# A conditioned transformer block: a second buffer for the turned blocks, the second MLP weight in four transfers, and the turning one step later on VectorE

## What is computed

```python
def rmsnorm(x, w):
    return x * rsqrt(mean(x * x, axis=-1, keepdims=True) + 1e-6) * w

def film(x, cond, w, b):
    scale, shift = split(cond @ w + b, 2, axis=-1)
    return x * (1.0 + scale[:, None, :]) + shift[:, None, :]

h = film(rmsnorm(x, norm1_w), cond, film1_w, film1_b)
Q, K, V = h @ q_w + q_b, h @ k_w + k_b, h @ v_w + v_b
attn = softmax(einsum('bnd,bmd->bnm', Q, K) * D ** -0.5)
x = x + (einsum('bnm,bmd->bnd', attn, V) @ proj_w + proj_b)
h = film(rmsnorm(x, norm2_w), cond, film2_w, film2_b)
out = x + gelu(h @ mlp_w1 + mlp_b1) @ mlp_w2 + mlp_b2      # hidden width 1024
```

## Time and profile before

| | |
|---|---|
| median of 3 runs | 243.05 us (243.01 to 243.99) |
| profiled execution, its own time | 245.84 us |
| its span | 244.1 us |
| PE busy | 222.2 us, 91% of the span |
| DVE busy | 140.1 us, 57% |
| ACT busy | 110.2 us, 45% |
| POOL busy | 70.1 us, 29% |
| granted TensorE clock, mean | 0.991 |
| DMA, over the span | 26.72 MB, 109 GB/s |

### The profile page before, as it was taken

One profiled execution on the slowest core, in us unless ns is written; L12 is line 12 of the kernel. 1 busy time (PEld: TensorE's weight loads), 2 busy tenths in 40 slices (PEclk: granted clock), 3 DMA queues, 4 the chain that ended last, 5 costly groups with the idle time before them and its releaser, 6 DMA issues.

```text
span 244.1 us, 3839 instructions
## 1 busy us (share of the span) xinstructions
PE 222.2 (91%) x1380; PEld 196.9 (81%) x1380; DVE 140.1 (57%) x276; ACT 110.2 (45%) x207; POOL 70.1 (29%) x102
## 2 busy tenths in 40 slices
PE   0987999998899996699999799999999999999994
PEld 0767888967778785699799689999999999999994
DVE  1498766666687863688888865224451454234223
ACT  3157653325433340444336558154746454644440
POOL 1575751004335110445524232510152025200000
PEclk9999999999999999799999999999999999999999
DMA  6993000065554594466466640000200020002002
GB/s 173 353 409 143 3 1 0 32 215 187 172 177 169 173 230 162 157 198 194 142 202 206 218 106 0 3 0 1 86 3 0 0 86 0 0 4 86 0 0 89
DMA packets 15282, 26.72 MB, mean 109 GB/s; under 512 B 1825, under 2 KB 10017, under 8 KB 15009
## 3 DMA queue, kind: packets, MB, share of 16 engines
q1 hardware_dynamic: 15264, 26.50, 33.3%
HBM read 16.00 MB, written 10.49 MB: 109 GB/s over the span
## 4 chain that ended last, share of the span: by engine, by line
PE 52%; DMA 26%; SPq 11%; DVE 6%; issue 3%; POOL 1%; ACT 0%; DVEq 0%; POOLq 0%
PE psum L690 24%; DMA crossing<-turned 23%; PE psum L805 19%; SPq L225 9%; PE psum L764 3%; DMA raw<-in_film_wT_dram 3%; PE psum L708 2%; PE psum L682 2%; PE psum L702 1%; SPq L187 1%; DVE hT L498 1%; DVE V_all L491 1%; DVE V_all L464 1%; DVE turned L588 1%; DVE row_max L577 1%
## 5 line engine op out<-in xcount | busy, mean ns | idle before, releaser
L764 PEld LDWEIGHTS psum<-V_all,probsT 128*128 128x128 f32 x384 | 48.2, 193 | 10.9 <-DVE probsT L595 10.3
L764 PE MATMUL psum<-V_all,probsT 128*128 128x256 f32 x384 | 49.9, 287 | 7.4 <-DVE probsT L595 7.4
L638 DVE TENSOR_TENSOR G_all<-probs,G_all 128x512 fp32r<-128x512 f32 x32 | 22.7, 710 | 53.3 <-ACT G_all L434 53.3
L805 PEld LDWEIGHTS psum<-w,G_all 128*128 128x128 f32 x384 | 49.6, 191 | 2.1
L805 PE MATMUL psum<-w,G_all 128*128 128x256 f32 x384 | 50.8, 283 | 0.0
L690 PE MATMUL psum<-hT,w 128*128 128x512 f32 (+1 forms) x192 | 49.4, 394 | 1.1 <-DVE hT L498 1.1
L690 PE MATMUL psum<-hT,G_all 128*128 128x512 f32 x192 | 46.7, 393 | 1.1 <-ACT probs L386 0.9
L434 ACT ACTIVATE probs<-psum,vcol 128x512 f32<-128x512 f32 x32 | 22.0, 688 | 49.6 <-PE psum L690 49.5
L386 ACT ACTIVATE probs<-psum,exp_bias 128x1024 f32<-128x1024 f32 x16 | 17.9, 1117 | 54.0 <-DVE exp_bias L580 54.0
L690 PEld LDWEIGHTS psum<-hT,G_all 128*128 128x128 f32 x192 | 35.0, 188 | 8.8 <-ACT probs L386 1.9
L690 PEld LDWEIGHTS psum<-hT,w 128*128 128x128 f32 x192 | 34.1, 189 | 7.0 <-issue 1.3
(11 more groups left out here) (60 smaller groups left out, 186.1 us busy)
## 6 DMA issues: line engine op xcount, KB each, us to landing
crossing<-turned SPq DMA_DIRECT2D x16, 512.0 KB, 3.6
keys_first<-crossing SPq DMA_DIRECT2D x64, 128.0 KB, 3.0
raw<-in_mlp_w_dram SPq DMA_DIRECT2D x2, 1024.0 KB, 7.5
out_dram<-x_rows SPq DMA_DIRECT2D x8, 256.0 KB, 2.1
x_rows<-in_x_dram SPq DMA_DIRECT2D x3, 512.0 KB, 9.3
raw<-in_film_wT_dram SPq DMA_DIRECT2D x2, 512.0 KB, 8.8
raw<-in_qk_weights_dram SPq DMA_DIRECT2D x2, 257.0 KB, 4.6
x_rows<-in_x_dram SPq DMA_DIRECT2D x2, 256.0 KB, 4.1
```

Of the source, the lines that this page charges most:

```text
L638: dve.tensor_tensor(gelu[:, m, LO, :], gelu_full[:, m % 2, :], gelu[:, m, HI, :].bitcast(F32), ALU.subtract).then_inc(gelu_ready, 1)
L764: last = pe.matmul(bank(6 + t % 2, D), probsT[:, t % 2, a, k, :], V_all[:, t // KT * KT + k, s, :], start=(n == 0), stop=(n == KT * len(PA ...
L805: last = pe.matmul(bank(4 + j, D), gelu[:, m, a, j * P:(j + 1) * P], w2[:, b, m, :], start=(m == 0 and n == 0), stop=(m == HT - 1 and n == ...
```

## The change

There are now two buffers for the turned blocks, used in turn: the old one for even tiles, and for odd tiles a part of raw that held the first film weight. turn_blocks(t) waits for store t-2 instead of t-1. The rows of the condition for the second norm, which stood in that part of raw, go to xn, and are loaded after the last transposes that read xn; where ScalarE wrote the squares of the first group to xn[0:2], they go to a half of h_full while the condition rows are in use. On VectorE, from step 2 on, turn_blocks(t-1) stands in step t, behind crossed_lo(t-3); the last turn follows the loop; the film products stand in steps 2 to 9 instead of 4 to 11. The second MLP weight is loaded in four quarters of 256 KB, each with its own semaphore, issued behind stores 5 to 8, ahead of the wait for the store's landing; each waits for the split of the quarter of the first weight whose place it takes.

```diff
@@ -85,7 +85,7 @@
         raw = sb("raw", [P, DT * (3 * D + KW + 4 * D)])
         probs = sb("probs", [P, 2, N])
         probsT = sb("probsT", [P, 2, 2, KT, P], F32R)
-        turned = sb("turned", [P, N])
+        turned_even = sb("turned", [P, N])
         keys_first = sb("keys_first", [P, 2, QT, KT, Q])
         crossing = nc.dram_tensor("crossing", [TILES, P, N], F32)
         xn = sb("xn", [P, GT, D])
@@ -118,8 +118,9 @@
         wqT, wkT = qk_raw[:, :, 0:D], qk_raw[:, :, D:]
         QK_END, VP_END = DT * (D + KW), at[0]
         film_wT = [weight(2 * D).rearrange("p t n -> p (t n)").rearrange("p (k d) -> p k d", d=D) for _ in range(2)]
-        cond_rows = [part.rearrange("p (r n) -> p r n", n=D) for part in (
-            keys_first[:, 0, :, :, :].rearrange("p a k n -> p (a k n)")[:, 0:B * D], raw[:, VP_END:VP_END + B * D])]
+        cond_rows = [keys_first[:, 0, :, :, :].rearrange("p a k n -> p (a k n)")[:, 0:B * D].rearrange(
+            "p (r n) -> p r n", n=D), xn[:, 0:B, :]]
+        turned = [turned_even[:, :], raw[:, VP_END:VP_END + N]]
         w1_raw, w2_raw = raw[:, 0:DT * H], raw[:, 0:HT * D]
         flat_probs = probs[:, :, :].rearrange("p a n -> p (a n)")
         bv_wide = flat_probs[:, 0:DT * P].rearrange("p (t n) -> p t n", t=DT)
@@ -139,7 +140,8 @@
             return psum[:, i, 0:w]
 
 
-        vec_in, wvp_in, rows_in, mlp_in = map(sem, ("vec_in", "wvp_in", "rows_in", "mlp_in"))
+        vec_in, wvp_in, rows_in, w1_in = map(sem, ("vec_in", "wvp_in", "rows_in", "w1_in"))
+        w2_in = [sem(f"w2_in{n}") for n in range(4)]
         wqk_in = [sem(f"wqk_in{e}") for e in range(DT)]
         film_in = [sem("film1_in"), sem("film2_in")]
         x_in = [sem(f"x_in{g}") for g in range(GROUPS)]
@@ -207,17 +209,18 @@
             load(film_wT[1], film2_wT, film_in[1])
 
             sp.wait_ge(addrow_done, 1)
-            load(w1_raw.rearrange("p (t n) -> p t n", t=DT), mlp_w1, mlp_in)
+            load(w1_raw.rearrange("p (t n) -> p t n", t=DT), mlp_w1, w1_in)
             sp.wait_ge(coef_ready, B)
+            sp.wait_ge(xT_done, GROUPS)
             load(cond_rows[1], rows[0:B, :].partition_broadcast(P), wide_in)
 
-
             for t in range(TILES):
-                if t == 7:
-                    sp.wait_ge(mlp_ready, 4)
-                    load(w2_raw.rearrange("p (t n) -> p t n", t=HT), mlp_w2, mlp_in)
                 sp.wait_ge(blocks_turned, t + 1)
-                sp.dma_start(crossing[t, :, :], turned[:, :]).then_inc(turned_out, 16)
+                sp.dma_start(crossing[t, :, :], turned[t % 2]).then_inc(turned_out, 16)
+                if 5 <= t < 9:
+                    sp.wait_ge(mlp_ready, t - 4)
+                    load(w2_raw[:, (t - 5) * 512:(t - 4) * 512].rearrange("p (t n) -> p t n", n=D),
+                         mlp_w2[:, (t - 5) * 2:(t - 4) * 2, :], w2_in[t - 5])
                 sp.wait_ge(turned_out, 16 * (t + 1))
                 if t >= 2:
                     sp.wait_ge(probsT_ready, t - 1)
@@ -304,12 +307,11 @@
                 pool.tensor_tensor(x_rows[:, t, :], x_rows[:, t, :], add_row[:, 0, :], ALU.add
                                    ).then_inc(residual_ready, 1)
                 if t == 0:
-                    pool.wait_ge(mlp_in, 16)
+                    pool.wait_ge(w1_in, 16)
                 if t < 4:
                     split_weights(w1_raw, w1_flat, t, 0)
-                if t == 6:
-                    pool.wait_ge(mlp_in, 32)
                 if 6 <= t < 10:
+                    pool.wait_ge(w2_in[t - 6], 16)
                     split_weights(w2_raw, w2_flat, t - 6, 4)
                 if t == 8:
                     inverse_rms(GROUPS)
@@ -397,12 +399,12 @@
                 act.copy(probsT[:, t % 2, HI, :, :].rearrange("p k (a n) -> p k a n", n=Q),
                          keys_first[:, t % 2, :, :, :].rearrange("p a k n -> p k a n")).then_inc(probsT_hi, 1)
 
-            def squares_after(g, tiles=range(GT)):
+            def squares_after(g, tiles=range(GT), place=lambda j: xn[:, j, :]):
 
                 act.wait_ge(rows_done, g * GT + GT)
                 act.wait_ge(xT_done, g + GROUPS)
                 for j in tiles:
-                    last = act.activation(xn[:, j, :], x_rows[:, ds(g * GT + j, 1), :].rearrange("p t n -> p (t n)"),
+                    last = act.activation(place(j), x_rows[:, ds(g * GT + j, 1), :].rearrange("p t n -> p (t n)"),
                                           ACT.Square, accum_out=sumsq[:, ds(g * GT + (TILES + j), 1)])
                 if GT - 1 in tiles:
                     last.then_inc(sq_done, 1)
@@ -419,7 +421,7 @@
                 if t == 0:
                     high_V(GROUPS - 1, range(2, GT))
                 if 8 <= t < 8 + GT:
-                    squares_after(0, (t - 8,))
+                    squares_after(0, (t - 8,), lambda j: h_full[:, 1, j * D:(j + 1) * D] if j < B else xn[:, j, :])
                 if t == TILES - 2:
                     columns_after(0, 4)
 
@@ -583,9 +585,9 @@
             def turn_blocks(t):
 
                 dve.wait_ge(exp_done, t + 1)
-                if t >= 1:
-                    dve.wait_ge(turned_out, 16 * t)
-                dve.transpose(turned[:, :].rearrange("p (q k n) -> p k q n", q=QT, k=KT),
+                if t >= 2:
+                    dve.wait_ge(turned_out, 16 * (t - 1))
+                dve.transpose(turned[t % 2].rearrange("p (q k n) -> p k q n", q=QT, k=KT),
                               probs[:, t % 2, :].rearrange("p (k q n) -> p k q n", k=KT, q=QT)
                               ).then_inc(blocks_turned, 1)
 
@@ -605,29 +607,29 @@
                                          in1=x_rows[:, t, :], op0=ALU.mult, op1=ALU.add).then_inc(rows_done, 1)
 
             for t in range(TILES):
-                if t == LAG - 1:
-                    crossed_lo(0)
                 row_maximum(t)
                 if t == 0:
                     low_V(GROUPS - 1, range(2))
-                if t >= LAG:
-                    crossed_lo(t - LAG + 1)
-                turn_blocks(t)
-                if t == 0:
+                    turn_blocks(0)
                     low_V(GROUPS - 1, range(2, GT))
                     group_terms(GROUPS - 1)
+                if t >= LAG - 1:
+                    crossed_lo(t - LAG + 1)
+                if t >= 2:
+                    turn_blocks(t - 1)
                 if t >= LAG:
                     add_attention(t - LAG)
-                if 4 <= t < 4 + 4 * DT:
-                    if t == 4:
+                if 2 <= t < 2 + 2 * DT * B:
+                    b, k = divmod(t - 2, 2 * DT)
+                    if t == 2:
                         dve.wait_ge(film_in[1], 16)
                         dve.wait_ge(wide_in, 32)
-                    b, k = divmod(t - 4, 2 * DT)
                     film_products(1, b, lambda n: h_full[:, 0, 0:D], (k,))
                     if k == 2 * DT - 1:
                         coefficients(1, b)
                 if t == TILES - 4:
                     normed_rows(GROUPS, 0)
+            turn_blocks(TILES - 1)
             low_columns(GROUPS, slice(0, GW))
             crossed_lo(TILES - 3)
             add_attention(TILES - 4)
```

## The result

The change took 240.39 us (median of 4 runs, 240.35 to 241.08); the kernel before took 243.52 in the runs of the same comparison (243.01 to 245.67). The ratio is 0.985, 95% interval 0.980 to 0.990: faster by 3.1 us in the medians (2.5 to 4.8 by the interval), where 7.0 were forecast. The profiled execution took 240.35 (span 238.5), 5.5 less than that of before. Medians here are over all runs of a kernel; the ratios leave out runs more than 1.5% above the kernel's fastest, which matters for the turn in its own step (3 of 6 runs in e3, 2 of 6 in e12), so that its ratios look better than its medians.

What follows compares the result with a forecast made beforehand. The prediction took TensorE (5.62 us a step) and the queue of stores and reads (5.73) as nearly equal bounds. A loop gain of 9.0 less 2.0 at the end gave 7.0 off the 243.05 median: 236.1, range 233.5 to 240.5.

Steps and rivals of the forecast that it cites:

- so I take the gain off the median: Whole kernel: the 7.0 gain, priced on a profiled execution of 245.84, was subtracted from the median 243.05, giving 236.1.
- Nothing was taken: SyncE queue, stores 5 to 8: weight pieces priced at no cost, with up to 1.2 us each kept for the range.
- A: SyncE queue: the weight quarters stand in the way, 1.2 us each, giving 239.7, or 241.0 with all 4.9; chance 0.11.
- C: SyncE queue: each weight quarter costs a whole trip in the chain, 12.8 us for four, giving 248.9; chance 0.02.
- the estimate of 6.0 us lost: Second MLP weight's load: by the skill's fit four quarters take 10.4 us, one whole 4.4, if in line; not followed.
- 5.4 to 5.9 a step: Loop over tiles: the path from turn to crossed_lo takes 10.8 to 11.8 us for two steps; 5.75 a step taken.
- Rival B: VectorE's wait for crossed_hi: the closed loop is long, slower than before above 6.57 us a step, giving 246.1; chance 0.06.
- the closed loop: Loop over tiles: turn, store, reads, landed keys, crossed_hi, crossed_lo, then the next turn, 10.8 to 11.8 us per two steps.
- a loss of 2.0 taken: Behind attention(11)'s start: late last turns delay tile 15's keys, so attention(15) ends later by 2.0 us, range 0 to 2.8.
- The 20.4 us that VectorE stood before its turns go: VectorE: its 20.4 us of waiting before turns disappears, since turn(t-1) in step t waits only for store(t-3).
- No cost: Condition rows loaded to xn: landed by 38.3, products reading them start after 53, so no time was charged.
- D: Loop over tiles: only the 4.53 stall and 1.4 of slow clock are gained, end costs 2.0, giving 239.1; chance 0.11.

Runs made afterwards that it cites:

- e3: The change with each tile's turn back in its own step, both buffers and the four weight pieces kept: 238.83 us, ratio to before 0.974.
- e12: Repeat, on another chip, of the change with each turn in its own step, both buffers and four pieces kept: 237.96 us, ratio to before 0.976.
- e8: The change with the later turn only in steps 2 and 3, each turn in its own step afterwards: 240.26 us, ratio to before 0.984.
- e2: The kernel before with only the second MLP weight's load cut into four; one buffer, turns in their own step: 238.44 us, ratio to before 0.983.
- e6: The change with turn(t-1) ahead of crossed_lo(t-3) instead of behind it, still one step late: 240.60 us, ratio to before 0.986.
- e5: The change with the last two turns, 14 and 15, in their own steps and none left behind the loop: 240.98 us, ratio to before 0.989.
- e11: Repeat, on another chip, of the kernel before with only the weight load cut into four: 239.96 us, ratio to before 0.987.
- e1: The kernel before, unedited, profiled again: median 242.85 us, ratio to before 0.999; the profiled execution took 241.93.

## Why the prediction was right in direction and wrong in size

**What bounds the kernel.** It named TensorE and the queue as nearly equal, and read the losses from TensorE's timeline of one execution. The runs show the queue as what holds the end: through turn(15) and the hidden layer with one buffer (3.23 after store(14)'s landing), through the keys of tile 15 in the change. The start of the row behind attention(15) is 9.83 after the issue of reads(15) there, 9.69 in the version with the whole weight, 9.70 with own-step turns, and about that wherever attention(15) waits, except in e8 (11.22), where attention(15) itself ran at the lower clock.

**The step that failed first: "so I take the gain off the median".** The 2.8 us by which the profiled execution exceeded the median were put down to stops "in both kernels". They were not in both: the change's profiled execution (240.35) lies on its median (240.39), while the kernel before, profiled again, had a loop 1.6 shorter and an end 1.8 shorter, so a part of the gain had been priced on stops that other executions of before do not have. Against its own execution the forecast was 7.0 and 5.5 came; against the medians only 3.1. Of the 3.9 us that are missing, some 2.3 are this step (245.84 less the median of 243.52), 0.7 the loop and 0.8 the end, below.

**The weight in four: right.** Nothing was taken, and the stores of e2 show nothing (3.60 to 3.73 beside 3.62). Rivals A and C fall. The Trainium skill (DMA: Bandwidth & Descriptors, Measured) has the rule to batch transfers to 1 MiB or more, from figures of GpSimd's path; the estimate of 6.0 us lost, worked out in the prediction from the same page's fit, did not come where nobody waits for the pieces at once: 4.3 and 3.5 us were won.

**The later turn: "5.4 to 5.9 a step", 5.75 taken.** Measured: (123.03 - 63.27 - 0.85) / 10 = 5.89, the upper end: from turn(3) to turn(11) two steps took 11.4 to 12.1, the longest turn(7) to turn(9) with 12.08, where 10.8 to 11.8 were summed. attention(1) was put at 64.0 and came at 63.27. So the loop's gain was 8.3 and not 9.0. Rival B's place was right, its size not (6.57 needed). But that the pace of the loop decides was the wrong view: e6 took the closed loop away and brought no time.

**The end: a loss of 2.0 taken, bounds 0 to 2.8.** 2.8 measured, and 4.6 against the second profile of before (24.85 to 20.3), whose end had no waits. The mechanism was the one named, keys of tile 15 later than TensorE wants them; reads(15) were expected 14.1 behind attention(11)'s start and came after 15.0. VectorE came 0.8 later into the last step, as the prediction allowed, store(14) landed in 2.90 instead of 3.65, and store(15) in 4.54 instead of 3.7. e5 shows that it is not the last turns that do it but the whole chain ahead of them.

**The second buffer.** "The 20.4 us that VectorE stood before its turns go" was right, and worth little in itself. What it brings with turns in their own step is the hidden layer free of store(14), and in the medians 2.0 us on one chip (e12 against e11) and nothing on another (e3 against e2); more runs would be needed to settle that. The later turn that came with it cost 2.9 on the chip on which both ran, through the queue's gaps and a late start.

**No cost** for the condition rows, as forecast: no wait for them, and store(0) left at 47.05 (47.56 before, 47.08 in e1). So 0.5 of the 8.3 was there ahead of the loop, and is not the change's.

**The rivals.** A's times (239.7, 241.0) lie nearest to 240.39, by luck: e2 shows that its mechanism did not happen. D's (239.1) is next, with its mechanism half right: the stall and the slow clock went, and much of the rest was given back, but at the end and not in the loop.

Left open: whether the load's place behind a store or its size of a quarter took the stall away, since no run has one without the other; how much of e6 and e8's missing gain is chance, since beside e12 their reads(15) leave 4.6 and 4.2 later, of which 1.6 and 2.3 are the later store(1) and the rest longer stores and issues of reads; and what the longer stops of single transfers are, such as the store that begins at 133.51 above. They are not quite irregular: the last store took 4.5 to 5.2 in five of the profiled executions with two buffers, and in three others (e5, e6, e8) the issue of the reads ahead of it 2.25 to 2.64 in place of 1.73.

## What to carry to other kernels

When a serial chain on one queue ends within some us of the busiest engine, follow that chain from its first issue to its last and price an edit by where the last link comes, not by the waits on the busy engine; those waits move elsewhere as long as the chain's end stays. This round trip through DRAM was shortened most by issuing the next store before the reads of the last; here the second buffer by itself brought 2 us on one chip and nothing on another, and 5 us over the weight in four with an order of the queue that uses it. And profile the kernel before twice, since one execution's own stops look like something to be won.

## What was not expected of the hardware

**A film product can take three times as long beside GpSimd.** Four of the eight products took 1.42 us in the change, one 0.70, the others 0.38 to 0.41; in the first profile of before all took 0.41 to 0.65. In VectorE's and GpSimd's timelines the long ones begin just behind a start of GpSimd's product on the weights, and end 0.3 after its end (64.69 + 1.29 = 65.98 and 64.84 + 1.42 = 66.26):

```profile
64.84 1.42 DVE L466 CUSTOM_DVE_ANT_0 h_full<-raw,xn 128x256 f32<-128x256 f32 x1
...
82.15 0.41 DVE L466 CUSTOM_DVE_ANT_0 h_full<-raw,xn 128x256 f32<-128x256 f32 x1
```

```profile
64.69 1.29 POOL L296 TENSOR_TENSOR w<-raw,w 128x512 fp32r<-128x512 f32 x1
```

The Trainium skill (SBUF — State Buffer, Who interferes with whom) says that a VectorE instruction with two SBUF inputs contends with a GpSimd instruction that reads SBUF, that the shared ports are an exclusive lock, and that the order of issue decides who blocks; the trace agrees, with 1.0 us more for each. The move to steps 2 to 9 alone does not do it: in e6, with the same steps but the turn ahead of crossed_lo, the eight took 0.38 to 0.59. One small wait of TensorE rests partly on it: attention(3) waited 0.21 for crossed_lo(3), which began at 73.66, behind the product of 70.48, though its high part was done at 72.95.

**A long wait of TensorE cost more than itself.** Behind the waits of 3.88 and 4.12, attention took 5.49 and 5.29 instead of 3.0, and 4.58 behind the one of 2.52; behind 2.28 in e8 it took 4.62, but behind 2.25 in e5 3.11. In the first of them the granted clock was 0.50, the lower level (columns: stretch, busy of five engines, PE first, granted clock, DMA share, GB/s):

```profile
93.70:97.40 3.70, 0.00 (x0) 0.00 (x0) 3.63 (x8) 1.05 (x2) 0.00 (x0) 0.91 0.87 280
...
99.00:101.00 2.00, 2.00 (x11) 2.00 (x11) 1.97 (x6) 0.00 (x0) 1.21 (x1) 0.50 0.82 238
```

Behind the waits of 1.0 to 1.7 in the change it stayed at full speed (2.4 GHz).
